# Layer norms of a small vision tower: half-sums on VectorE ahead of one product with the matrix of ones, instead of two accumulated products

## The reference

```python
def _layernorm(x, axis=-1, eps=1e-05):
    m = jnp.mean(x, axis=axis, keepdims=True)
    v = jnp.var(x, axis=axis, keepdims=True)
    return (x - m) / jnp.sqrt(v + eps)

h = _L0_tok_ref(x, ...)
h = h + _L0_attn_ref(_layernorm(h), ...)
h = h + _L0_ffn_ref(_layernorm(h), ...)
h = h + _L1_attn_ref(_layernorm(h), ...)
h = h + _L1_ffn_ref(_layernorm(h), ...)
```

## Time and profile before

| | us |
|---|---|
| runs | 1218.44, 1225.39, 1233.18 |
| profiled execution, its own time | 1225.06 |
| its span | 1223.2 |
| TensorE busy, matmul | 986.1 (81%) |
| VectorE busy | 732.1 (60%) |
| ScalarE busy | 441.7 (36%) |
| GpSimd busy | 279.0 (23%) |

### The profile page before, as it was taken

The page is one execution under the profiler, slowest core; times in us unless marked ns, Lnnn a source line. Parts: engine busy times, 40 slices in busy tenths (PEclk is TensorE's granted clock), DMA queues, the critical chain, the costliest instruction groups (busy, mean ns, idle before and its releaser), DMA issues.

```text
span 1223.2 us, 17495 instructions
## 1 busy us (share of the span) xinstructions
PE 986.1 (81%) x5925; PEld 613.7 (50%) x5926; DVE 732.1 (60%) x1131; ACT 441.7 (36%) x880; POOL 279.0 (23%) x361
## 2 busy tenths in 40 slices
PE   8985272876787778775989999998999998549996
PEld 6763230422232223221667777775777766326664
DVE  2545733699889988988535444444767776303332
ACT  1227450544464445420341222224444343223332
POOL 5905800112121212100000000004543540231222
PEclk9998655668776877767999999999999999669999
DMA  6283478122112211135163121100000000342321
GB/s 224 93 323 110 110 209 207 34 45 44 43 26 45 44 42 27 28 104 209 35 264 99 41 79 41 40 0 1 2 1 1 0 1 1 148 149 71 87 78 35
DMA packets 92704, 96.05 MB, mean 79 GB/s; under 512 B 64350, under 2 KB 78687, under 8 KB 90976
## 3 DMA queue, kind: packets, MB, share of 16 engines
q1 hardware_dynamic: 89904, 87.91, 23.6%
q0 software_dynamic: 2736, 7.30, 1.6%
HBM read 61.57 MB, written 34.59 MB: 79 GB/s over the span
## 4 chain that ended last, share of the span: by engine, by line
PE 65%; ACT 11%; DVE 8%; issue 7%; SPq 4%; DMA 3%; POOL 1%; another core or an unknown queue 0%; ACTq 0%; DVEq 0%; POOLq 0%
PE ps L523 8%; PE ps L582 7%; ACT mem L1529 7%; PE ps L1106 6%; PE ps L1077 4%; PE ps L999 4%; PE ps L1386 4%; PE ps L1402 4%; PE ps L1297 3%; DVE mem L1820 3%; PE ps L1231 3%; PE ps L392 3%; PE ps L400 2%; SPq L761 2%; PE ps L1115 2%
## 5 line engine op out<-in xcount | busy, mean ns | idle before, releaser
L1832 DVE TENSOR_TENSOR mem<-mem,ps 128x1024 f32<-128x1024 f32 x144 | 175.0, 1216 | 58.4 <-PE ps L1090 58.4
L1529 ACT ACTIVATE mem<-ps 128x512 f32<-128x512 f32 x288 | 158.6, 597 | 121.1 <-PE ps L1077 96.1
L1077 PE MATMUL ps<-mem 64*128 64x128 bf16 x1144 | 116.0, 265 | 77.4 <-ACT mem L1529 76.4
L1820 DVE TENSOR_TENSOR mem<-mem 128x1024 f32<-128x1024 f32 x144 | 175.4, 1218 | 2.7 <-ACT mem L1529 2.7
L956 POOL TENSOR_TENSOR mem<-mem,sm 128x296 f32<-128x296 f32 x128 | 87.6, 718 | 361.1 <-ACT mem L1607 318.2
L1077 PEld LDWEIGHTS ps<-mem 64*128 64x128 bf16 x1144 | 69.3, 112 | 155.6 <-ACT mem L1529 116.3
L935 POOL TENSOR_SCALAR mem<-mem,sm 128x16 f32<-128x16 f32 x148 | 76.1, 536 | 295.4 <-PE ps L1106 295.4
L1090 PE MATMUL ps<-mem 64*128 64x512 bf16 x296 | 91.9, 486 | 49.7 <-DVE mem L1832 41.2
L1106 PE MATMUL ps<-mem 128*32 128x512 f32 x592 | 115.1, 865 | 0.0
L523 PE MATMUL ps<-mem 128*128 (+1 forms) x384 | 109.5, 416 | 0.6 <-DVE mem L496 0.6
L582 PE MATMUL ps<-mem 128*128 128x296 f32 x352 | 100.6, 415 | 1.9 <-DVE mem L645 1.9
(11 more groups left out here) (222 smaller groups left out, 1548.0 us busy)
## 6 DMA issues: line engine op xcount, KB each, us to landing
mem<-gates SPq DMA_DIRECT2D x7, 1184.0 KB, 6.0
mem<-in_w SPq DMA_DIRECT2D x2, 4096.0 KB, 17.5
slots<-mem SPq DMA_DIRECT2D x1, 6682.0 KB, 23.5
mem<-slots SPq DMA_DIRECT2D x26, 257.0 KB, 2.7
mem<-in_patches SPq DMA_DIRECT2D x7, 864.0 KB, 4.5
mem<-factor_rows SPq DMA_DIRECT2D x296, 16.0 KB, 1.8
mem<-factor_rows SPq DMA_DIRECT2D x37, 128.0 KB, 2.3
mem<-delta_rows SPq DMA_DIRECT2D x9, 512.0 KB, 4.5
```

The source lines that it names most:

```text
L1077: mm = nc.tensor.matmul(ps[:, r, e * BT:(e + 1) * BT], a_stat[64 * r:64 * r + 64, g, e, :], delta_in[b % 2][64 * r:64 * r + 64, g, :], sta ...
L1529: nc.scalar.activation(decay_slots[b % 2][:, :, 4 * k:4 * k + 4], ps[:, k % 2, :].rearrange("p (e t) -> p t e", e=4), ACT.Exp).then_inc(de ...
L1820: nc.vector.tensor_tensor(now[:, gs], now[:, gs], before[:, gs], ALU.mult).then_inc(multed, 1)
L1832: nc.vector.tensor_tensor(now, now, got, ALU.add).then_inc(added, 1)
```

## The change

For each chunk of each layer norm, VectorE adds the two halves of h into a buffer `hsum` of 296 columns (`dve_sum`), and the two halves of the squares in place (`dve_fold`). TensorE then makes one product instead of two for the mean, and one for the variance. There are 4 x 8 = 32 chunks in all. The waits change with it: `pe_mean` waits for `summed` instead of for the addition that wrote h; `pe_var` waits for `folded` instead of `squared`. `dve_sum` waits for VectorE's own last addition, and for the mean before (one buffer). `dve_fold` waits for ScalarE's square. In `pe_moe` the variance moves from j == 8 to j == 9.

```diff
+        hsum = home(16112, CH)
...
         def pe_mean(pe, s, c, bank, deep=1):
-            h = hF0 if s == "scan" else hF
+            pe.wait_ge(LN["summed"], LN_FROM[s] + c + 1)
             pe.wait_ge(LN["centered"], LN_FROM[s] + c + 3 - deep)
-            for k in range(HALVES):
-                mm = nc.tensor.matmul(ps[:, bank, 0:CH], ones[:], h[:, k, ds(c * CH, CH)],
-                                      start=(k == 0), stop=(k == HALVES - 1))
-            mm.then_inc(LN["mean"], 1)
+            nc.tensor.matmul(ps[:, bank, 0:CH], ones[:], hsum, start=True, stop=True).then_inc(LN["mean"], 1)

         def pe_var(pe, s, c, j, bank, deep=1):
-            pe.wait_ge(LN["squared"], LN_FROM[s] + c + 1)
+            pe.wait_ge(LN["folded"], LN_FROM[s] + c + 1)
             pe.wait_ge(LN["logvar"], LN_FROM[s] + c + 3 - deep)
-            for k in range(HALVES):
-                mm = nc.tensor.matmul(ps[:, bank, 0:CH], ones[:], sq[:, j, k, :],
-                                      start=(k == 0), stop=(k == HALVES - 1))
-            mm.then_inc(LN["var"], 1)
+            nc.tensor.matmul(ps[:, bank, 0:CH], ones[:], sq[:, j, 0, :],
+                             start=True, stop=True).then_inc(LN["var"], 1)
...
+        def dve_sum(dve, s, c, ready, n):
+            h = hF0 if s == "scan" else hF
+            dve.wait_ge(ready, n)
+            dve.wait_ge(LN["mean"], LN_FROM[s] + c)
+            nc.vector.tensor_tensor(hsum, h[:, 0, ds(c * CH, CH)], h[:, 1, ds(c * CH, CH)],
+                                    ALU.add).then_inc(LN["summed"], 1)
+
+        def dve_fold(dve, s, c, j):
+            dve.wait_ge(LN["squared"], LN_FROM[s] + c + 1)
+            nc.vector.tensor_tensor(sq[:, j, 0, :], sq[:, j, 0, :], sq[:, j, 1, :],
+                                    ALU.add).then_inc(LN["folded"], 1)
```

Where VectorE's two new calls stand, stage by stage:

```diff
 # experts of layer 0 (pe_moe, dve_moe)
-                    if on(1) and j == 8:
+                    if on(1) and j == 9:
                         pe_var(pe, ln, c - 1, 1 - cj, 0)
...
                     if on(1) and j == 5:
                         dve_center(dve, ln, c - 1, 0)
+                    if on(1) and j == 7:
+                        dve_fold(dve, ln, c - 1, 1 - cj)
                 if on(1):
                     dve_scale(dve, ln, c - 1, 1 - cj)
                 dve.wait_ge(s["down"], c + 1)
                 cs = ds(c * CH, CH)
                 nc.vector.tensor_tensor(hF[:, :, cs], ...)
+                dve_sum(dve, ln, c, s["h"], c + 3)
...
 # embedding (dve_embed): after the two additions of chunk k
+                    dve_sum(dve, ln, k, embedded, k * 2 + 6)
                 if on(1):
+                    dve_fold(dve, ln, k - 1, 1 - j)
                     dve_scale(dve, ln, k - 1, 1 - j)
...
 # down-projection (dve_down)
             def dve_down(k, j, on):
+                if on(2):
+                    dve_fold(dve, ln, k - 2, j)
                 if on(0):
...
                 if on(1):
                     dve_center(dve, ln, k - 1, 0)
+                if on(0):
+                    dve_sum(dve, ln, k, scan_h, k + 3)
                 if on(2):
                     dve_scale(dve, ln, k - 2, j)
...
 # attention: add_projected (in p == 1), and the head of dve_step
+                dve_sum(dve, ln, c, attn_h, c + 1)
...
             def dve_step(c, cj, p, more2, more1):
+                if p == 3 and not (isinstance(c, int) and c == 0):
+                    dve_fold(dve, ln, c - 1, 1 - cj)
                 if more1 or p < 3:
                     soften(*ahead(c, cj, p, 1))
```

More of the change, by code:

```diff
@@ L284, in build @@
         embedded_ps, embedded = sem("embedded_ps"), sem("embedded")
-        LN = {n: sem(f"ln_{n}") for n in ("mean", "centered", "squared", "var", "logvar", "rstd", "normed")}
+        LN = {n: sem(f"ln_{n}") for n in ("summed", "mean", "centered", "squared", "folded", "var", "logvar", "rstd", "normed")}
         LN_FROM = {"scan": 0, "moe0": NCH, "attn": 2 * NCH, "moe1": 3 * NCH}
@@ L558, in norm_mean @@
             def norm_mean(c):
-                pe.wait_ge(s["h"], c + 3)
                 pe.wait_ge(LN["logvar"], LN_FROM[ln] + c + 2)
@@ L1014, in pe_embed @@
                 if on(1):
-                    pe.wait_ge(embedded, k * 2 + 4)
                     pe_mean(pe, ln, k - 1, 4)
@@ L1162, in pe_down @@
                 if on(1):
-                    pe.wait_ge(scan_h, k + 2)
                     pe_mean(pe, ln, k - 1, 0)
@@ L1311, in pe_step @@
                 if p == 2 and not (isinstance(c, int) and c == 0):
-                    pe.wait_ge(attn_h, c)
                     pe_mean(pe, ln, c - 1, 7)
@@ L1332, in pe_last @@
                 project(NCH - 1, 1)
-                pe.wait_ge(attn_h, NCH)
                 pe_mean(pe, ln, NCH - 1, 7)
@@ L1990, in dve_last @@
                 dve_center(dve, ln, NCH - 1, 7)
+                dve_fold(dve, ln, NCH - 1, 1)
                 dve_scale(dve, ln, NCH - 1, 1)
```

## The result

A gain of 10 us was forecast and none came. The changed kernel's median is 1236.89 us (4 runs, 1232.99 to 1245.33) against 1221.91 us for the kernel before (4 runs): a ratio of 1.0117, 95% interval [1.0075, 1.0159]. Forecast were 1214.8 us and a range up to 1226.

What follows compares the result with a forecast made beforehand. TensorE was taken as the bound nearly everywhere, a closed VectorE-ScalarE loop in the down-projection. Embedding -1.1, down-projection +4.3, experts -6.9, attention -6.7 gave -10.4 us: 1214.8 us, own range 1209 to 1220, 8 in 10 from 1205 to 1226.

Steps and rivals of the forecast that it cites:

- The slack of 0.15 us: Attention: scale_outputs ends 0.15 us before TensorE needs it, so the fold is covered; each 0.1 us short costs 0.7.
- the slower-side rival: Attention: the fold blocks VectorE and its wait for the square reaches TensorE; +17.5 us in full, 1239; chance 0.06.
- the forecast's own terms, -7.0 and +0.1: Attention: 7 chunks save two products each, -7.0 us; the last chunk's norm, a bare chain, adds +0.1.
- Forecast +4.3 us: Down-projection: the fold lengthens a closed loop of VectorE and ScalarE; first step +0.6, six steps +2.5, end +1.2.
- the third rival: Down-projection: TensorE's clock falls to 1.2 GHz through idle time in each step; +11 us, 1226; chance 0.10.
- Forecast -1.1 us: Embedding in all: steady steps -5.1, first step +1.1, GpSimd's interference +3.0, and a further -0.1.
- The first step: Embedding, first step with a norm: no up-projection covers the variance's wait, which leaves +1.1 us.
- The steady step: Embedding: the mean's product is saved whole, the variance waits 0.1 to 0.2 us; 6 full steps x 0.85 = -5.1.
- forecast +3.0: Embedding: GpSimd holds up ten VectorE additions with two SBUF inputs, taken at 0.3 us each.
- The discount: Embedding: GpSimd's delay taken as 0.3 us per addition, not near 0.45, since part falls where TensorE still works.
- GpSimd blocks the embedding: Embedding: the ten additions cost as much as in the worst row, 16.5 us instead of 3.0; 1228.3; chance 0.13.
- The bare chains: Last chunks' norms of experts and attention: two additions with handovers in, two products out, +0.1 us each.

Runs made afterwards that it cites:

- e13: The changed kernel plus seven products that nobody reads in TensorE's gaps between experts and attention; ratio to the kernel before 0.9978 [0.9942, 1.0014].
- e1: The changed kernel with the embedding's layer norm put back to two products, no sum or fold there; ratio to the kernel before 1.0007 [0.9952, 1.0062].
- e4: The changed kernel with GpSimd's preparation of constants started only when all chunks are embedded; 1257.75 us, only the embedding's steps can be read.
- e14: The changed kernel unaltered, run again on the same chip as its variants; ratio to the kernel before 1.0029 [0.9983, 1.0076].
- e10: The kernel before with only the experts' norm changed, the other three with two products; stretch between experts and attention 49.3 us.
- e5: The changed kernel with the fold moved earlier in VectorE's order in embedding and down-projection; ratio to the kernel before 0.9952 [0.9911, 0.9994].

## Why the prediction was wrong

**Experts: right.** A chunk takes 24.92 us (25.91 before), without a gap; of the 7 us that this makes, 0.85 went to a transfer of the gates ahead of the first chunk (5.00 us against 4.15), which the change does not touch. The sum and the fold are hidden, as said:

```profile
769.69 0.47 DVE L428 TENSOR_TENSOR mem<-mem 128x296 f32 x1
...
783.43 0.46 DVE L434 TENSOR_TENSOR mem<-mem 128x296 f32<-128x296 f32 x1
```

**Attention: right chunk by chunk, not at its ends.** Forecast were 24.0 us a chunk. In the chain of the changed kernel, the mean's and the variance's product of two neighbouring chunks:

```profile
942.35 0.69 PE ps L392 x2
948.62 0.70 PE ps L397 x2
...
966.42 0.69 PE ps L392 x2
972.69 0.70 PE ps L397 x2
```

24.07 us. The slack of 0.15 us held, so the slower-side rival is out. The stage gained 3.1 us, not 6.7 (the forecast's own terms, -7.0 and +0.1, add to -6.9), and the missing 3.6 have two parts. TensorE's clock falls in the last chunk, which has no next one beside it; e13 has the same code there, the clock held, and the stage took 156.3 us instead of 158.6, so the fall costs 2.3. The other 1.3 are at the two ends: by the starts of the output projections the interval of the first chunk became only 0.4 us shorter (23.44 against 23.87) and that of the last one in e13 by 0.1 (13.16 against 13.23), where the five between gave 0.96 each. Windows of the changed kernel there:

```profile
1037.00:1041.00 4.00, 2.27 (x32) 2.10 (x32) 1.42 (x4) 1.91 (x5) 0.00 (x0) 0.90 0.00 0
1041.00:1045.00 4.00, 3.11 (x11) 1.89 (x10) 1.60 (x5) 1.20 (x4) 0.00 (x0) 0.50 0.00 0
```

and the kernel before at the same work (2.62 of 4 busy, no fall):

```profile
1030.00:1034.00 4.00, 2.62 (x30) 2.02 (x30) 0.83 (x4) 1.29 (x4) 0.00 (x0) 1.00 0.00 0
```

**Down-projection: the size was right, the clock on top of it was not in it.** Forecast +4.3 us; e1 measured +4.1, and from scale to scale its steps are 4.53 and 4.76 us in turn, where before they were 4.15 and 4.39: the 4.6 us forecast in the mean. The changed kernel took 44.9 or 45.0 us in all of its four profiles (first, e4, e13, e14), +6.2 to +6.9 against the three of before, with the clock falling twice in the stage:

```profile
602.00:606.00 4.00, 3.66 (x8) 1.50 (x9) 2.74 (x6) 1.84 (x4) 0.00 (x0) 0.66 0.00 0
...
626.00:630.00 4.00, 2.88 (x7) 1.01 (x8) 1.72 (x3) 1.95 (x4) 0.00 (x0) 0.65 1.04 451
630.00:634.00 4.00, 3.41 (x8) 0.52 (x7) 0.77 (x1) 1.36 (x3) 0.00 (x0) 0.50 1.01 434
```

That is the third rival, in part: it was priced at +11 as if the clock stayed down for all steps, and these four took 2.8 us more than e1. Not all of that is the two falls: they also began the stage at 0.50 for 5.7 to 5.9 us, e1 for 3.0, and with two products and 5.8 us at 0.50 e10 took 39.4 us instead of 38.1. The step that failed is that the rival was kept out of the sum at 0.10, although the same sum gave TensorE 1.4 us of idle time a step. Why e1 alone kept its clock is not shown.

**Embedding: the step that failed most.** Forecast -1.1 us, measured +6.2; the second execution stands +5.0 to +7.0 against the three of before. Taken apart with the seventh mean product (five steady steps behind the first):
- The first step: forecast +1.1. In e4, without GpSimd, 8.87 us from the first mean to the second, before 7.81: +1.06. Right.
- The steady step: forecast -0.85, measured -0.55 (9.28 against 9.83 in the means of five). The idle time in front of the variance is 0.16 us, as said, but TensorE's stream is broken by it. In the changed kernel it is 2.92 us from the start of the up-projection to the first product behind the variance, in e5, where nothing waits, 2.49: a wait of 0.16 costs 0.43.

```profile
64.54 2.16 PE L1038 MATMUL ps<-mem 128*128 x8
...
65.96 0.47 DVE L428 TENSOR_TENSOR mem<-mem 128x296 f32 x1 [0.26 <-DVE mem L1751]
66.35 0.46 DVE L434 TENSOR_TENSOR mem<-mem 128x296 f32<-128x296 f32 x1
...
66.86 0.77 PE L397 MATMUL ps<-mem,ones 128*128 128x296 f32 x2 [0.16 <-DVE mem L434]
...
67.46 0.73 PE L1012 MATMUL ps<-mem 128*128 128x288 f32 x2
```

- GpSimd: forecast +3.0, measured +8.8. The prediction read an average of 0.45 us for each of ten instructions and took 0.3, "since part falls where TensorE still works". The average was near: the ten additions were held 5.5 us in sum, 0.55 each. The discount was wrong, for all of it reached TensorE, and the fall of the clock behind it, 3.0 us, was in no term. This was the rival "GpSimd blocks the embedding" at about half of its price, given 0.13.

**The bare chains: a term of 0.1 us each.** Each was priced by additions against products only. What it costs depends on whether the clock falls: 0.2 us between the stages in e13, with its fillers, where it held, up to 5.8 where it fell. The same code came out either way in the kernel before.

**Sum.** -1.1 + 4.3 - 6.9 - 6.7 was forecast; the first changed execution gave, from the table, +6.2 + 6.9 - 5.9 + 1.8 - 3.1 = +5.9, and the scan and the rest +3.8, in code that the change does not touch, to +9.7. The experts and the chunks of attention, where nothing new waits, were right; the wrong terms have one cause in common: new idle time of TensorE was priced at its length, without what the clock does behind it, 3.0 us in the embedding, up to 2.8 in the down-projection, 1.8 and 2.3 at the two bare chains. Beside that stands the discount on GpSimd's term, 2.5 us. And the place of the two calls was taken as given. With the fold placed where VectorE was idle (e5), the same change gains in the embedding 6 to 8 us where the forecast had 1.1 and costs nothing in the down-projection where it had 4.3.

## What to carry to other kernels

Work moved from a busy engine to a freer one pays only where the new instruction starts long before its result is wanted; ask of each added instruction where in its engine's order the engine was idle anyway, not only how long it takes. Price new idle time of TensorE with the fall of its clock behind it, above all in chains between two stages where nothing runs beside, and look at what GpSimd is doing at that very instant when a VectorE instruction with two SBUF inputs goes on the critical path. When the time of untouched code differs by more than the change is worth, compare by stage, in several executions.

## What the hardware showed that was not expected

- An addition of 128x296 on VectorE takes 0.46 to 0.47 us alone and 2.37 to 2.38 us if it starts just behind a GpSimd TENSOR_TENSOR of 128x1024, at whose end it is let go. Behind the start of GpSimd's TENSOR_SCALAR (L913, 2.84 us) it is let go earlier: it ended 1.43 us after that start, in the changed kernel (46.42 and 47.85) and in e5 (52.95 and 54.38).
- A wait of 0.16 us ahead of a product cost TensorE 0.43 us of its stream.
- TensorE's clock fell without a long gap: no idle time of TensorE in the 5 us ahead of the falls at 603 and 627 us of the changed kernel was over 1.85 us, and none ahead of the one at 849 us over 0.90.
- VectorE's sum, inside a loop, starts 0.26 us behind the additions whose end it waits for (29.31 against 29.04 in e4's loop); the same pair ahead of the loop has 0.03 us between (20.05 against 20.02).
- The granted clock fell or held behind the same gaps of TensorE in executions of the same kernel (43.8, 43.8 and 48.8 us for the same stretch), and it held in both profiles of kernels with seven products that nobody reads in these gaps.
